# Scan stage of a Mamba and mixture-of-experts kernel: softplus sums, row means and GpSimd's waits rearranged

## What is computed

```python
x_ssm, x_gate = split(x @ in_proj_w.T + in_proj_b)
x_conv = silu(conv1d(x_ssm, 4 taps) + conv_b)
B, C = split(x_conv @ bc_w.T + bc_b)              # 16 states each
dt = softplus(x_conv @ dt_w.T + dt_b)
h = h * exp(dt * A) + dt * B * x_conv             # over 512 steps, 16 states per channel
y = (sum over the states of h * C + x_conv * D) * silu(x_gate)
z = norm(y @ out_w.T + out_b + x) * ln_g + ln_b
x1 = norm(x + z)                                  # then routing and experts
out = norm(x1 + experts(x1))
```

## Time and profile before

| | |
|---|---|
| median of 3 runs | 1302.05 us (1300.89 to 1302.22) |
| profiled execution | 1299.35 us, span 1297.5 us |
| TensorE busy | 1155.2 us (89%) |
| VectorE busy | 1046.1 us (81%) |
| ScalarE busy | 867.1 us (67%) |
| GpSimd busy | 765.0 us (59%) |

### The profile page before, as it was taken

The page is one execution under the profiler, slowest core; times in us unless marked ns, Lnnn a source line. Parts: engine busy times, 40 slices in busy tenths (PEclk is TensorE's granted clock), DMA queues, the critical chain, the costliest instruction groups (busy, mean ns, idle before and its releaser), DMA issues. The chain is left out here.

```text
span 1297.5 us, 17895 instructions
## 1 busy us (share of the span) xinstructions
PE 1155.2 (89%) x5150; PEld 800.0 (62%) x5150; DVE 1046.1 (81%) x1804; ACT 867.1 (67%) x1511; POOL 765.0 (59%) x571
## 2 busy tenths in 40 slices
PE   8879798989889898785969999999999999999960
PEld 4324353434343433255868888888888888888850
DVE  4999898999998999988647777777777777777754
ACT  4675768594958686535646777776777776777744
POOL 0466668998988897986634444334444334443353
PEclk9899998999999998898989999999999999999985
DMA  3543435454554544545756656666656666566638
GB/s 118 201 168 132 174 130 189 162 193 176 176 191 152 198 162 166 217 167 201 261 170 169 143 147 167 164 155 167 141 151 165 167 155 168 133 159 164 168 41 267
DMA packets 69259, 217.20 MB, mean 167 GB/s; under 512 B 7520, under 2 KB 43232, under 8 KB 56288
## 3 DMA queue, kind: packets, MB, share of 16 engines
q1 hardware_dynamic: 33888, 171.61, 37.4%
q0 software_dynamic: 26880, 36.72, 16.4%
q10 hardware_dynamic: 8448, 8.39, 2.0%
HBM read 165.54 MB, written 51.15 MB: 167 GB/s over the span
## 5 line engine op out<-in xcount | busy, mean ns | idle before, releaser
L1106 DVE TENSOR_TENSOR_SCAN state<-decay,p_bu 128x512 f32<-128x512 f32 x256 | 297.1, 1201 | 0.1
L662 PE MATMUL p_y<-read,small 128*128 128x512 f32 x512 | 251.2, 627 | 49.8 <-POOL read L1299 49.7
L1648 POOL DMA_INDIRECT total<-o_v,tok x144 | 251.3, 1745 | 39.6 <-issue 39.3
L662 PEld LDWEIGHTS p_y<-read,small 128*128 128x128 f32 x512 | 98.0, 198 | 190.7 <-issue 109.5
L1646 POOL TENSOR_TENSOR scrap<-neg_half 128x1 f32<-128x1 f32 x36 | 23.2, 645 | 313.0 <-ACT o_v L1560 310.5
L512 ACT ACTIVATE gate_v<-p_g,bias 128x512 f32<-128x512 f32 x144 | 98.6, 685 | 136.7 <-PE p_up L502 132.3
L520 DVE TENSOR_SCALAR up_v<-up_v 128x512 f32<-128x512 f32 x144 | 68.9, 478 | 147.0 <-ACT up_v L515 144.7
L861 ACT ACTIVATE decay<-dt,scan_rate 128x511 f32<-128x511 f32 x256 | 162.8, 710 | 6.3 <-DVE state L1106 6.1
L1359 POOL DMA_INDIRECT queues<-rows,index x128 | 130.3, 1018 | 34.6 <-issue 32.9
L1299 POOL TENSOR_TENSOR read<-state,bc 128x1024 f32<-128x1024 f32 x64 | 127.7, 2001 | 31.2 <-DVE p_u L1088 15.5
L533 ACT ACTIVATE ah<-a_v 128x512 fp32r<-128x512 f32 x144 | 91.2, 634 | 57.0 <-DVE a_v L526 57.0
(11 more groups left out here) (237 smaller groups left out, 2984.1 us busy)
## 6 DMA issues: line engine op xcount, KB each, us to landing
bc<-bc_rows SPq DMA_DIRECT2D x32, 1024.0 KB, 4.7
first_raw<-in_w_experts SPq DMA_DIRECT2D x19, 1668.0 KB, 7.9
raw_w<-in_w_experts SPq DMA_DIRECT2D x18, 1668.0 KB, 7.6
first_wh<-bc_rows SPq DMA_DIRECT2D x16, 1024.0 KB, 4.7
first_wl<-bc_rows SPq DMA_DIRECT2D x16, 1024.0 KB, 4.7
first_rows<-queues SPq DMA_DIRECT2D x19, 544.0 KB, 3.6
xq<-queues SPq DMA_DIRECT2D x18, 544.0 KB, 3.6
queues<-pad SPq DMA_DIRECT2D x9, 544.0 KB, 5.1
```

Source lines behind the costliest of these rows:

```text
L662: mm = pe.matmul(p_y[h][:, :], ident[:, :], read[:, t % 4, h, :], start=False, stop=(t == SLOTS - 1))
L1106: dve.tensor_tensor_scan(state[t % 4][:, h, :], decay[(SLOTS * s.n + t) % AHEAD][:, h, :], p_bu[:, h * LEN:(h + 1) * LEN], 0.0, ALU.mult, ...
L1648: pool.indirect_dma_start(total, bass.IndirectOffsetOnAxis(ap=tok[t.p][:, a:a + 1], axis=0), o_v[t.p][:, a, :], None, compute_op=ALU.add). ...
```

## The change

Seven things change, all in the scan stage.

1. GpSimd's second sum (`add_log` of GpSimd) goes. VectorE adds the logarithm to `relu` in slot 13 of rounds 0 to 6, just ahead of dt; the function was there for the first round.
2. GpSimd's softplus sum moves from slot 11 to slot 10.
3. The three waits above go: products 8, 12 and 14 wait for the input products of their slot alone.
4. ScalarE computes the two scaled row sums (`neg_16th`, `neg_mean`) itself, at the head of `variance`; GpSimd's `mean` goes.
5. ScalarE's order: decays 10, 11 and 12 move to slots 5, 6 and 9, so that none lies in slots 7 and 8; the table of Exp is loaded right behind the gate's silu; the copy of the B and C rows (`store_bc`) moves behind the first Exp of the softplus. `load_table` gets scale=0.0.
6. TensorE issues the count matmuls in slot 2, ahead of the skip and the first state sum, and not in slot 3.
7. GpSimd's first scatter of a round moves behind product 7.

```diff
-                if r.d and r.b and t == 3:
+                if r.d and r.b and t == 2:
                     count(r)
...
             act.activation(flat(expo[:, :, :]), flat(expo[:, :, :]), ACT.Exp, scale=-1.0).then_inc(s_exp, 1)
+            store_bc(r)
...
+        def variance(r, which):
+
+            s = r.s.at(-1)
+            if which == 0:
+                for b in range(2):
+                    bank, n = r.block(f"o{b}")
+                    act.wait_ge(bank_read[bank], n)
+            else:
+                act.wait_ge(s_residual, s.n + 1)
+            act.activation(neg_16th[:, which, :], row_sum[:, which, :], ACT.Copy, scale=-1.0 / (16 * D))
+            act.activation(neg_mean[:, which, :], row_sum[:, which, :], ACT.Copy, scale=-1.0 / D).then_inc(s_mean, 1)
             act.wait_ge(s_mean, 2 * s.n + which + 1)
...
-        DECAYS = {0: (2,), 1: (3,), 2: (4, 5), 3: (6,), 4: (7, 8), 5: (9,), 6: (10,), 7: (11,), 8: (12,), 10: (13,),
+        DECAYS = {0: (2,), 1: (3,), 2: (4, 5), 3: (6,), 4: (7, 8), 5: (9, 10), 6: (11,), 9: (12,), 10: (13,),
                   12: (14,), 13: (15,)}
...
+                    if r.b:
+                        silu_gate(ROUNDS[ROUNDS.index(r) - 1])
+                        load_table(ACT.Exp)
...
+                if r.a and r.b and t == 13:
+                    add_log(r)
                 if r.a and t == 13:
                     scan_inputs(r)
...
-            if r.c and t == 9:
-                pool.wait_ge(s_residual, r.s.at(-1).n + 1)
-            if r.a and t == 13:
-                pool.wait_ge(s_dt, r.s.at(1).n + 1)
-            if r.a and t == 15:
-                pool.wait_ge(s_u, r.s.at(1).n + 1)
...
-                if r.a and r.b and t == 11:
+                if r.a and r.b and t == 10:
                     softplus_rest(r)
-                if r.a and r.b and t == 12:
-                    add_log(r)
+                if r.d and r.b and t == 8:
+                    scatter(r.s.at(-2), BEHIND_READ)
```

More of the change, by code:

```diff
@@ L767, in load_table @@
         def load_table(func):
-            act.activation(table[:, :], table[:, :], func).then_inc(s_table, 1)
+            act.activation(table[:, :], table[:, :], func, scale=0.0).then_inc(s_table, 1)
         act.wait_ge(s_set_dve, 1)
@@ L884, in take_out @@
             last.then_inc(done, 1)
-        def variance(s, which):
+        def variance(r, which):
[8 more added lines that the diff above has]
+            act.activation(neg_mean[:, which, :], row_sum[:, which, :], ACT.Copy, scale=-1.0 / D).then_inc(s_mean, 1)
             act.wait_ge(s_mean, 2 * s.n + which + 1)
@@ L943, in act_stage1 @@
                         load_table(ACT.Exp)
+                if r.b and not r.a and t == 7:
+                    silu_gate(ROUNDS[ROUNDS.index(r) - 1])
                 if r.a and t == 9:
@@ L950, in act_stage1 @@
                     store_in(r, t - 9)
-                if r.b and t == 7:
-                    silu_gate(ROUNDS[ROUNDS.index(r) - 1])
                 if r.like == Round.FIRST and t == SLOTS - 1:
@@ L983, in act_stage1 @@
                 if r.c and r.b and t == 5:
-                    variance(r.s.at(-1), 0)
+                    variance(r, 0)
                 if r.c and r.b and t == 6:
@@ L996, in act_stage1 @@
                     store_dt(r, 1)
-                    store_bc(r)
                 if r.c and r.b and t == 11:
-                    variance(r.s.at(-1), 1)
+                    variance(r, 1)
                 if r.c and r.b and t == 13:
@@ L1305, in softplus_rest @@
             pool.tensor_tensor(rest[:, :, :], rest[:, :, :], expo[:, :, :], ALU.add).then_inc(s_rest, 1)
[L1307 to L1323, removed]
         def power(s, which):
@@ L1360, in scatter @@
                                         rows[s.p][:, i // TOPK, :], None).then_inc(s_scat[s.p], 16)
-        SCATTERS = {8: (0,), 9: (1, 2), 10: (3,), 13: (4,)}
+        BEHIND_READ = (0,)
+        SCATTERS = {9: (1, 2), 10: (3,), 13: (4,)}
         BEHIND_DRIVE = (5, 6)
-        NEXT_TO_LAST = {8: (0,), 9: (1, 2), 10: (3,), 11: (4, 5), 12: (6,)}
+        NEXT_TO_LAST = {9: (1, 2), 10: (3,), 11: (4, 5), 12: (6,)}
         LAST_SCATTERS = {13: range(TT * TOPK)}
@@ L1401, in pool_stage1 @@
                     scatter(r.s.at(-3), LATE_SCATTERS[t])
-                if r.c and r.b and t == 5:
-                    mean(r, 0)
                 if r.b:
@@ L1428, in pool_stage1 @@
                     scale(r)
-                if r.c and r.b and t == 10:
-                    mean(r, 1)
                 if r.c and r.b and t == 12:
```

## The result

The changed kernel takes 1322.3 us (median of 4 runs, 1317.3 to 1326.8), the kernel before 1301.5 (1299.9 to 1302.2) beside it: 1.0150 times the time, 95% interval 1.0127 to 1.0172. It is slower by 20.8 us where 10.2 was forecast, and 1322 lies outside the range of 1285 to 1317. Its profiled execution has a span of 1320.5 us.

A forecast was written before the change was run, and what follows sets the result against it. VectorE's queue was taken to bound the first 560 us. Terms -18.5 + 8.9 + 11.4 + 12.8 - 3.2 - 1.2 = +10.2 us on the median 1302.05 gave 1312; range 1285 to 1317, the forecast's own 1306 to 1316.

The forecast's parts named there:

- GpSimd's product in slot 15: Slot 15: product 14, no longer waiting for u, starts first and holds drive; +1.83 x 7 = +12.8 us.
- The step that I trusted least: Slot 15: who comes first, product 14 or drive; forecast the product, by a lead of 0.06 us.
- rival A: Slot 15: drive gets in ahead of product 14, giving -2.6 us, 1299.5; chance 0.14.
- rival B: Slots 13 and 15: VectorE held in neither, -14.0 us, 1288, or 1279 if the residual is free too; chance 0.26.
- rival D: More loss: further product or pow in slot 13, TensorE's clock falling, or slot 12's decays late; 1316 to 1322, chance 0.06.
- Wait for GpSimd's sum: Ahead of dt: VectorE's waits in 7 places for GpSimd's second sum go; -18.5 us.
- the added sum: Slot 13: VectorE adds the logarithm itself ahead of dt; 1.27 x 7 = +8.9 us.
- a product in slot 13: Slot 13: a GpSimd product, freed from the wait for dt, holds VectorE; +1.63 x 7 = +11.4 us.
- One product either way: Slot 13: also with GpSimd late in scatter rounds, one product lies ahead of the sum or between; +1.63 per round.
- Count sooner: Count matmuls issued a slot sooner on TensorE, so VectorE's waits for them go; -3.2 us.
- Residual, row means, scatter: Residual asks sooner, row means delay the norm, product 7 goes ahead of the scatter; residual held 1.2, not 1.5; -1.2 us.
- Decays, table loads, B and C rows: ScalarE's reordered work is hidden by its idle 19 of 68 us: nothing; up to 9 us if slot 12's decays came late.

The follow-up runs named there:

- Experiment 1: Changed kernel with the wait for u put back ahead of product 14, nothing else; 1293.2 us, 0.9936 of the kernel before.
- experiment 9: Changed kernel with all three waits back, the residual's ahead of product 7 instead of 8, first scatter ahead of product 7 again; 1294.0 us, 0.9938.
- experiment 11: Changed kernel, three waits back: residual's ahead of product 7, dt's ahead of product 11; first scatter ahead of product 7, slot 13's a slot sooner; 1285.5 us.
- experiment 6: Kernel before with its wait for u taken away, nothing else; 1326.6 us, 1.0200.
- experiment 5: Changed kernel with six matmuls of zeros per scanned round on TensorE, three ahead of each wait for products 13 and 15; 1317.9 us, 1.0128.
- experiment 2: Changed kernel with the wait for dt put back ahead of product 12, nothing else; 1315.2 us, 1.0109 of the kernel before.
- Experiment 8: Kernel before with the logarithm added by VectorE in slot 13, GpSimd's second sum gone, all three waits kept; 1296.0 us, 0.9956.
- experiment 7: Kernel before with the count matmuls issued in slot 2, nothing else; 1300.5 us, 0.9999.
- experiment 3: Changed kernel with the wait for the residual put back ahead of product 8, nothing else; 1317.1 us, 1.0122 of the kernel before.

## Why the prediction was wrong

The direction was right and the size was not: +10.2 forecast, +20.8 measured. In the profile the scan stage ends 18.5 us later, 1.5 of them from a later first scan, which the kernels of experiments 1, 9 and 11 do not have though they hold most of the change. In the points below the slots of the changed kernel hold several effects at once, so they do not add up.

- **GpSimd's product in slot 15: +12.8 forecast, +12.6 measured.** The step that I trusted least held in seven rounds of seven, with a drive of 3.03 us for the 3.1 that was worked out and a lead of 0.05 us. Rivals A and B fall with it.
- **What else that product does: 0 forecast, about +13 measured.** This is the step that failed. The prediction charged the lost wait for u with VectorE's stop alone; what follows from the stop stood only in rival D, with a chance of 0.06. Experiment 1 puts the whole price behind the first scan at 25.7 us of the stage, 13.1 over the stop itself, and experiment 6, from the other kernel, at 19.9, 7.3 over it. The stop holds back the next input products, product 15 and TensorE's state sums. At the end of round 2 TensorE so idles 3.1 us where it had idled 1.6, and its clock falls to half. By experiment 5 some 7 us of the 13 are the clock's. The other 6 are argued to be the later start, which no run shows by itself. Rival D named the clock as one of three ways to 1316 to 1322; its time was nearly right, but the clock is about half of what it has to explain, and the other two (slot 12's decays late, a further product or a pow in slot 13) did not happen.
- **Wait for GpSimd's sum, the added sum, and a product in slot 13: -18.5 + 8.9 + 11.4 = +1.8 forecast, -3.8 measured.** Slot 13 undisturbed is 5.81 us (experiment 2, round 0). Over seven rounds that makes 40.7, against 51.1 in the kernel before: so the wait's end and the added sum come to -10.4, where -9.6 was forecast. The holding was the one term of the sum that was much too large: 6.6 us and not 11.4. "One product either way" is right in rounds 0 and 1 alone (1.7 to 1.85 each); in the others the sum is held 0.6 by the tail of product 11, and dt goes ahead of a pow. Only six rounds of the kernel before have a held pow (1.90 to 1.93 us), and not the seven of rival B; and such a pow holds nothing when it comes first (experiment 2). Experiment 8 has the gain by itself, at -6.0.
- **Count sooner: -3.2 forecast, -1.5 in slot 3 measured.** With u's wait back it is -3.7, as forecast, and -3.7 with the matmuls of zeros too, so the rest was the clock's. But by experiment 7 the move alone brings nothing, so the reason given, that the waits come off the time, did not hold by itself. The forecast of this term was in part lucky.
- **Residual, row means, scatter: -1.2 forecast, +6.2 in slot 9 measured.** With u's wait back it is -1.5. The forecast was for a round in which the norm's chain comes in time, and in three rounds it no longer did. The removal of the residual's own wait was put at nothing where GpSimd is late anyway; experiment 3 puts it at 1.8 us in slot 9 and 1.8 in slot 13 (round 1, where GpSimd is then in time for dt to go ahead of product 12).
- **Decays, table loads, B and C rows: 0.** VectorE's waits for decays are 1.2 us in all, all of it ahead of the first scan. Right, with the idle time of TensorE ahead of the B and C matmuls gone as said.

Of the two pages of the Trainium skill that the prediction weighed, the one with the exclusive lock (SBUF — State Buffer, Who interferes with whom) is borne out: issue order decided in all seven slots 15, by 0.05 us. The other (Perfetto Trace Analysis, Per-engine timelines) puts a VectorE row's start at its arithmetic; here a row begins while the operation still stands, as the drive's does at 376.19 with its end at 379.22. So in such rows the start is near that of the request; the two starts that were compared ordered all seven pairs rightly.

## What to carry to other kernels

A wait on one engine's queue may be what gives the other engine the memory first: before taking it out, look at what both engines would start in that instant, and charge the loser with the whole of the winner's instruction, or of several where they are issued back to back. Then follow the stop one engine further. Here VectorE lost 12.6 us by it and the kernel 26 to 29 us, in part because TensorE idled longer behind it and came back at half its clock.

## What the hardware did that I had not expected

- A VectorE operation with two operands in SBUF that asked during a GpSimd product didn't get in ahead of a second product that followed at once: 3.62 us for an operation of 1.23, held through the rest of both (3.94 us together). A small operation that followed as closely did not keep it out. What makes the difference is not shown.
- GpSimd's operations of 4 elements per partition are held just as the large ones are, 1.06 and 2.03 us for 0.20 and 1.04. But the pow of this size, started first, held no one: VectorE's sum took 1.21 us from the midst of it.
- A lead of 0.05 us decided seven rounds of seven, with durations of 3.030 to 3.033 us.
- At the end of round 2, 3.1 us of idle TensorE were followed by a granted clock of 0.50 to 0.53 over some 13 us, where 1.6 us of it at the same place left it at 1.00. In the kernel of experiment 6 the same 3.1 us at the same place were followed by only 3.4 us at half the clock.
